# Pooled residual moved from VectorE to ScalarE and GpSimd, and TensorE's loop turned, in a window attention block on one core

## The chip, the core and the metric

The kernel runs on one core of one Trainium2 chip. The metric is the device time of one execution in microseconds. All data is float32. Five engines run side by side, each with its own instruction stream, and meet only through semaphores: TensorE (matmuls into PSUM), VectorE, ScalarE, GpSimd (which here touches SBUF only) and SyncE, which issues the loads and stores.

## What is computed

The input x is 4 x 128 x 96 x 96. It is normalised by groups (32 groups of 4 channels), passed through a multi-scale linear attention within windows of 4 x 4 pixels, and added to itself:

```python
qkv = jnp.einsum('nchw,oc->nohw', xw, qkv_w)       # xw: windows of 4 x 4 pixels
pooled = _avg_pool5(qkv)                           # 5 x 5 mean inside the window
msq = jnp.concatenate([qkv, pooled], axis=1)       # full and pooled branch
q = relu(msq[..., :DIM]); k = relu(msq[..., DIM:2 * DIM]); v = msq[..., 2 * DIM:]
v = jnp.pad(v, ..., constant_values=1.0)           # a column of ones: the denominator
kv = jnp.einsum('ngld,nglm->ngdm', k, v)
out = jnp.einsum('ngld,ngdm->nglm', q, kv)
out = out[..., :-1] / (out[..., -1:] + 1e-15)
y = jnp.einsum('nchw,oc->nohw', out, proj_w)       # then batch norm, scale and shift
x = x + y
```

A 5 x 5 mean inside a 4 x 4 window has only 3 x 3 different values (corners and edges repeat), so the pooled branch is computed on 9 pixels a window instead of 16 and spread out at the very end.

## The kernel before

The image is cut into 96 strips (NS) of 4 rows and 96 columns: 384 pixels (SP), 24 windows, and 216 pooled pixels (SPP). Channels lie on the 128 partitions. The whole input lies in SBUF (x_all), and the result is written over it strip by strip, then stored. Every engine runs its own list over the strips. Those of VectorE, ScalarE and GpSimd are written out for all 96 strips; TensorE's is a loop (line 664) over two strips a round, s = 1, 3, ... 93, with strips 0 and 95 ahead of it and behind it.

TensorE's step for strip s (lines 638 to 651), in this order: kv_products full and pooled (line 582; 48 and 32 matmul passes on 64 x 32 tiles of the array), conv_q (lines 556 and 558), conv_kv of strip s+1 (line 538), transposes of strip s-1 (line 627), conv_kv_pooled of s+1 (line 549), project of s-1 (lines 633 and 635), out_products full and pooled (line 611). Each float32 matmul appears as two passes, each with its weight load.

ScalarE's step (lines 343 to 356): relu of q full and pooled (lines 312, 318), relu of the next k (line 286), evacuation of the transposed outputs o_sb (lines 325, 332), the masked copies of the next v, four full and, behind the relu of the pooled k (line 292), six pooled ones (line 305). The last of the six signals vm_p, for which the pooled kv products wait, together with num_f.

VectorE's step (line 479): own_heads for both branches (line 446, kvc_full and kvc_pool, 2 x 2 instructions), in some strips the statistics of the next image (line 377), residual of strip s-1 (lines 449 to 464), divide for both branches (lines 472, 473, 476; it signals num_f and num_p). residual adds the full part from PSUM bank 0 in one instruction (line 452), and then the pooled part from PSUM bank 1 in four (line 462), one for each pair of kinds of rows and columns. The last signals y_done, for which the store on SyncE waits, and the full kv products two strips on, since they write banks 0 and 1.

GpSimd's step (line 236): the normalisation of strip s+2 into xn (lines 255, 256), which waits for conv_q of strip s (the same half of xn), and eight additions that pool it into xp (line 234).

Of the kernel before, what the change touches and what calls it, by code (L numbers as in the profile page):

```python
# [65 lines left out]
def build(nc, x, wq, wkv, proj, bn, consts, out):  # L66
# [20 lines left out]
    with ExitStack() as ctx:  # L87
# [46 lines left out]
        o_sb = sb("o_sb", [SP + SPP])  # L134

# [42 lines left out]
        added_f = sem("added_f")  # L178
        y_done = sem("y_done")
# [4 lines left out]
        def col(i, n=1):  # L184
            return cst[:, i:i + n]
# [24 lines left out]
        def _(sp):  # L210
# [16 lines left out]
        def _(pool):  # L227
# [51 lines left out]
            over_strips(step)  # L279

        @block.scalar
        def _(act):
# [12 lines left out]
            def masked_v(s, pooled):  # L295
# [37 lines left out]

            def square_root(n):
# [8 lines left out]
            def step(s, b, at, phase):  # L343
# [20 lines left out]
            pooled_out(NS - 1)  # L364

        @block.vector
        def _(dve):
# [48 lines left out]

            dve.memset(dev[:], 0.0).then_inc(y_done, 1)
# [31 lines left out]
            def residual(s):  # L449
# [4 lines left out]
                dve.wait_ge(y_p, s + 1)  # L454
                dve.wait_ge(added_f, s + 1)
                src = ps[:, Y_P, 0:SPP].rearrange("p (w r c) -> p w r c", r=NP, c=NP)
                dst = xs.rearrange("p (r w c) -> p w r c", r=WS, c=WS)
                ends, ends_p, mid, mid_p = slice(0, WS, WS - 1), slice(0, NP, NP - 1), slice(1, 3), slice(1, 2)
                for rows, rows_p in ((ends, ends_p), (mid, mid_p)):
                    for cols, cols_p in ((ends, ends_p), (mid, mid_p)):  # L460
                        part = dst[:, :, rows, cols]
# [67 lines left out]
        def _(pe):  # L529
# [12 lines left out]
            def conv_kv_pooled(s, p):  # L542
                pe.wait_ge(xp_ready, s + 1)

                wait(pe, qm_f, s)
# [16 lines left out]
            def kv_products(s, pooled):  # L562


                k, vm, tiles, wins, bank, done = (
                    (k_pool, vm_pool, TP, EP, KVP, kv_p) if pooled else (k_full, vm_full, TF, EF, KVF, kv_f))
                pe.wait_ge(km_p if pooled else km_f, s + 1)
                pe.wait_ge(vm_p if pooled else vm_f, s + 1)
                if pooled:

                    wait(pe, num_f, s)
                else:

                    wait(pe, y_done, s)

                pe.nop(nofuse=True)
                n = wins * KC
                for t in range(tiles):
                    for r in range(G):
                        rows = slice(H64 * r, H64 * (r + 1))  # L580
                        for i in range(4):
                            last = pe.matmul(ps[Q4 * i:Q4 * (i + 1), bank + r, t * n:(t + 1) * n],  # L582
                                             k[rows, t, Q4 * i:Q4 * (i + 1)], vm[rows, t, :, i, :],
                                             start=True, stop=True)
                last.then_inc(done, 1)

            def out_products(s, pooled):


                q, kvc, done, bank, tiles, wins = (  # L590
                    (q_pool, kvc_pool, out_p, OUTP, TP, WP) if pooled else
                    (q_full, kvc_full, out_f, OUTF, TF, WF))
                pe.wait_ge(qm_p if pooled else qm_f, s + 1)
                pe.wait_ge(kvc_p if pooled else kvc_f, s + 1)
                if not pooled:

                    pe.wait_ge(kvc_p, s + 1)
                elif not is_last(s):

                    pe.wait_ge(km_f, s + 2)  # L600
                    pe.wait_ge(vm_f, s + 2)
                pe.nop(nofuse=True)
                n = QG * KC
                blocks = q[:].rearrange("p n e j -> p n (e j)")
                for t in range(tiles):
                    for e in range(wins):
                        for g in range(G):
                            rows = slice(H64 * g, H64 * (g + 1))
                            for c in range(4):
                                r, w = c // QG, t * QG * wins + c % QG * wins + e  # L610
                                last = pe.matmul(ps[Q4 * c:Q4 * (c + 1), bank + g, t * n:(t + 1) * n],  # L611
# [85 lines left out]
```

## Time and profile before

| | us |
|---|---|
| median of 3 runs (from 928.78 to 931.36) | 930.72 |
| the profiled execution | 930.24 |
| its span, from first to last instruction | 928.3 |

The page gives for each engine its busy time and its share of the span. Busy is not the same as needed: TensorE's matmuls are pipelined and their ends are modelled, so that small gaps count more than the share suggests. PE is TensorE's matmul side, PEld its weight load side, DVE is VectorE, ACT ScalarE, POOL GpSimd. The weight load of the next matmul runs beside the matmul before it. The span has three parts: some 69 us in which the first loads, the first statistics and the first three strips run, 92 regular strips, and about 14 us of the last strip. In the timeline a row begins with its start in us and its duration; where the engine stood idle before it, the time and what ended it follow in brackets ("issue": nothing that the profile shows).

### The profile page before, as it was taken

Reading aid. Unit: us, or ns where it says so; the run is one execution under the profiler, and the core shown is the slowest. Engines: PE = TensorE matmul, PEld = TensorE weight load, DVE = VectorE, ACT = ScalarE, POOL = GpSimd, SP = SyncE. Lnnn points to the kernel's source line nnn. Section 1 sums busy time; section 2 is a strip of 40 time slices with the busy share of each in tenths; the row PEclk is TensorE's granted clock in tenths of the full one; section 3 lists DMA queues with packets and bytes.
Section 4 is the critical chain, followed back from the end, with each engine's and each line's share of the span. In section 5 each row is a group of like instructions: output and inputs, shape, how many; then the busy total and the mean of one; then the engine's idle time right before and its main releaser. Section 6 shows DMA issues by size and latency. Waiting matters only on the chain.

```text
span 928.3 us, 65376 instructions
## 1 busy us (share of the span) xinstructions
PE 873.8 (94%) x29282; PEld 733.4 (79%) x29282; DVE 772.3 (83%) x1625; ACT 609.5 (66%) x1542; POOL 456.0 (49%) x967
## 2 busy tenths in 40 slices
PE   0689999999999999999999999999999999999997
PEld 0578888888888888888888888888888888888885
DVE  7369989998878898998878998999887878787886
ACT  0457676767676767676766667676767676767673
POOL 1545454545454545555554545454545454545550
PEclk9999999999999999999999999999999999999998
DMA  9910000000000000000000000000000000000000
GB/s 378 431 50 17 26 17 26 17 26 17 25 19 25 26 17 26 17 26 17 26 17 26 18 26 17 26 17 27 17 26 17 25 25 18 26 17 26 18 26 27
DMA packets 15893, 38.77 MB, mean 42 GB/s; under 512 B 1888, under 2 KB 14688, under 8 KB 15456
## 3 DMA queue, kind: packets, MB, share of 16 engines
q1 hardware_dynamic: 15840, 38.26, 10.6%
q14 instruction: 44, 0.36, 0.1%
q8 instruction: 9, 0.15, 0.1%
HBM read 19.38 MB, written 18.87 MB: 41 GB/s over the span
## 4 chain that ended last, share of the span: by engine, by line
PE 93%; issue 3%; DVE 2%; POOL 1%; DMA 0%; ACT 0%; DVEq 0%; POOLq 0%
PE ps L611 23%; PE ps L582 19%; PE ps L538 14%; PE ps L549 9%; PE ps L556 9%; PE ps L633 7%; PE ps L627 6%; PE ps L635 4%; PE ps L558 4%; DVE stats L377 1%; DMA x_all<-x 0%; POOL hs L234 0%; DVE kvc_full L446 0%; POOL xp L234 0%; ACT o_sb L325 0%
## 5 line engine op out<-in xcount | busy, mean ns | idle before, releaser
L255 POOL TENSOR_TENSOR xn<-x_all,mean_t 128x384 f32<-128x384 f32 x96 | 79.4, 827 | 393.6 <-PE ps L558 375.1
L305 ACT ACTIVATE vm_pool<-ps,cst 128x256 f32<-128x256 f32 x576 | 225.5, 543 | 0.4 <-PE ps L549 0.4
L446 DVE TENSOR_TENSOR kvc_full<-ps,cst 128x864 f32<-128x864 f32 x192 | 193.7, 1050 | 17.8 <-PE ps L582 17.6
L446 DVE TENSOR_TENSOR kvc_pool<-ps,cst 128x864 f32<-128x864 f32 x192 | 193.2, 1048 | 0.0
L305 ACT ACTIVATE vm_full<-ps,cst 128x384 f32<-128x384 f32 x384 | 192.2, 598 | 0.9 <-PE ps L538 0.9
L312 ACT ACTIVATE q_full<-ps 128x384 f32<-128x384 f32 x96 | 47.2, 491 | 208.5 <-PE ps L556 208.5
L538 PE MATMUL ps<-wkv_sb,xn 128*128 128x128 f32 x1152 | 145.5, 276 | 23.5 <-POOL xn L256 23.5
L538 PEld LDWEIGHTS ps<-wkv_sb,xn 128*128 128x128 f32 x1152 | 144.1, 193 | 23.5 <-issue 23.5
L452 DVE SCALAR_TENSOR_TENSOR x_all<-ps,shift,x_all 128x384 f32<-128x384 f32 x96 | 59.3, 618 | 93.4 <-PE ps L633 93.2
L611 PEld LDWEIGHTS ps<-kvc_full,q_full 64*32 64x32 f32 x9216 | 99.5, 105 | 26.4 <-issue 26.3
L611 PE MATMUL ps<-kvc_pool,q_pool 64*32 64x72 f32 x9216 | 115.8, 230 | 2.1 <-issue 2.1
L611 PE MATMUL ps<-kvc_full,q_full 64*32 64x72 f32 x9216 | 116.5, 230 | 0.9 <-issue 0.9
L582 PE MATMUL ps<-vm_full,k_full 64*32 64x144 f32 x4608 | 95.8, 289 | 21.5 <-issue 20.7
L611 PEld LDWEIGHTS ps<-kvc_pool,q_pool 64*32 64x32 f32 x9216 | 101.5, 105 | 6.7 <-issue 2.4
L549 PE MATMUL ps<-wkv_sb,xp 128*128 128x128 f32 x768 | 102.5, 277 | 0.6 <-POOL xp L234 0.6
L549 PEld LDWEIGHTS ps<-wkv_sb,xp 128*128 128x128 f32 x768 | 94.1, 193 | 0.9 <-POOL xp L234 0.9
L582 PE MATMUL ps<-vm_pool,k_pool 64*32 64x216 f32 x3072 | 94.1, 350 | 0.3
L582 PEld LDWEIGHTS ps<-vm_full,k_full 64*32 64x32 f32 x4608 | 69.5, 106 | 31.5 <-issue 29.2
L234 POOL TENSOR_TENSOR hs<-ht,xn 128x96 f32<-128x96 f32 x192 | 85.6, 446 | 15.1
L556 PE MATMUL ps<-xn,wq_sb 128*128 128x384 f32 x192 | 88.4, 542 | 0.0
L256 POOL TENSOR_TENSOR xn<-xn,rstd_t 128x384 f32<-128x384 f32 x96 | 79.6, 829 | 7.6
L325 ACT ACTIVATE o_sb<-ps 128x384 f32<-128x384 f32 x96 | 47.2, 491 | 53.2 <-PE ps L627 53.2
(66 smaller groups left out, 1242.2 us busy)
## 6 DMA issues: line engine op xcount, KB each, us to landing
out<-x_all SPq DMA_DIRECT2D x96, 192.0 KB, 1.9
x_all<-x SPq DMA_DIRECT2D x3, 4608.0 KB, 32.1
x_all<-x SPq DMA_DIRECT2D x6, 768.0 KB, 8.1
cst<-consts SPq DMA_DIRECT2D x1, 172.0 KB, 11.0
wkv_sb<-wkv SPq DMA_DIRECT2D x1, 128.0 KB, 10.8
o_sb<-proj SPq DMA_DIRECT2D x1, 128.0 KB, 10.4
wq_sb<-wq SPq DMA_DIRECT2D x1, 64.0 KB, 10.5
bn_sb<-bn SPq DMA_DIRECT2D x1, 2.0 KB, 10.3
```

Of the source, the lines that this page charges most:

```text
L234: return pool.tensor_tensor(o, a, b, ALU.add)
L255: link(pool.tensor_tensor(xr, src, mean, ALU.subtract), 1)
L256: pool.tensor_tensor(xn[:, p], xn[:, p], rstd, ALU.mult).then_inc(xn_ready, 1)
L305: last = act.activation(heads[:, :, e, :, 0:D], src, ACT.Copy, scale=col(mask + e))
L446: last = dve.tensor_tensor(kvc[:, g], src.to_broadcast(shape), own, ALU.mult)
L452: dve.scalar_tensor_tensor(xs, ps[:, Y_F, 0:SP], shift[:], xs, ALU.add, ALU.add).then_inc(added_f, 1)
L538: last = pe.matmul(ps[:, bank, t * P:(t + 1) * P], xn[:, p, t * P:(t + 1) * P], wkv_sb[:, half * P:(half + 1) * P], start=True, stop=True)
L549: last = pe.matmul(ps[:, bank, t * P:(t + 1) * P], xp[:, p, t * P:(t + 1) * P], wkv_sb[:, half * P:(half + 1) * P], start=True, stop=True)
L556: pe.matmul(ps[:, Q_F, 0:SP], wq_sb[:], xn[:, p], start=True, stop=True).then_inc(q_f, 1)
L582: last = pe.matmul(ps[Q4 * i:Q4 * (i + 1), bank + r, t * n:(t + 1) * n], k[rows, t, Q4 * i:Q4 * (i + 1)], vm[rows, t, :, i, :], start=True ...
L611: last = pe.matmul(ps[Q4 * c:Q4 * (c + 1), bank + g, t * n:(t + 1) * n], blocks[rows, 4 * t + c, Q4 * e:Q4 * (e + 1)], kvc[rows, r, w], st ...
L633: pe.matmul(ps[:, Y_F, 0:SP], projT[:, 0:P], o_sb[:, 0:SP], start=True, stop=True).then_inc(y_f, 1)
```

## The change

Three things change.

1. The pooled part of the residual leaves VectorE. ScalarE copies PSUM bank 1 (128 x 216) to a new tile y_pool, between the second and the third pooled masked v activation of its step, and signals y_copied. GpSimd then makes the four additions, behind the normalisation in its step, and signals y_done. y_pool is a single buffer: the copy waits for y_done of the strip before.
2. TensorE waits for added_f and y_copied instead of y_done where banks 0 and 1 are written again. Some waits that others imply are dropped.
3. TensorE's loop begins with the next strip's conv_kv and ends with its conv_q; the kv products and conv_q of strip 0 stand ahead of the loop. The cyclic order of the matmuls is the same.

```diff
@@ sync
-                    sp.wait_ge(y_done, t + (b * SPB + 2))
+                    sp.wait_ge(y_done, t + (b * SPB + 1))
@@ gpsimd
+            def residual_pooled(s):
+                pool.wait_ge(added_f, s + 1)
+                pool.wait_ge(y_copied, s + 1)
+                src = y_pool[:].rearrange("p (w r c) -> p w r c", r=NP, c=NP)
+                dst = x_all[:, s * SP:(s + 1) * SP].rearrange("p (r w c) -> p w r c", r=WS, c=WS)
+                ends, ends_p, mid, mid_p = slice(0, WS, WS - 1), slice(0, NP, NP - 1), slice(1, 3), slice(1, 2)
+                for rows, rows_p in ((ends, ends_p), (mid, mid_p)):
+                    for cols, cols_p in ((ends, ends_p), (mid, mid_p)):
+                        part = dst[:, :, rows, cols]
+                        last = add(part, src[:, :, rows_p, cols_p].to_broadcast([P, NW, 2, 2]), part)
+                last.then_inc(y_done, 1)
...
                     normalise_and_pool(s + 2, s % 2)
+                if not is_first(s):
+                    residual_pooled(s - 1)
@@ scalar
                 for e in range(wins):
                     last = act.activation(heads[:, :, e, :, 0:D], src, ACT.Copy, scale=col(mask + e))
+                    if between is not None and e == 1:
+                        copy_y_pooled(between)
                 last.then_inc(done, 1)
...
+            def copy_y_pooled(s):
+                act.wait_ge(y_p, s + 1)
+                wait(act, y_done, s)
+                act.activation(y_pool[:], ps[:, Y_P, 0:SPP], ACT.Copy).then_inc(y_copied, 1)
...
-                    masked_v(s + 1, True)
+                    masked_v(s + 1, True, None if is_first(s) else s - 1)
@@ vector
-                dve.wait_ge(y_p, s + 1)
-                dve.wait_ge(added_f, s + 1)
...
-                        last = dve.tensor_tensor(part, src[:, :, rows_p, cols_p].to_broadcast([P, NW, 2, 2]),
-                                                 part, ALU.add)
-                last.then_inc(y_done, 1)
@@ tensor
             def conv_q(s, p):
-                pe.wait_ge(km_p, s + 1)
...
-                pe.wait_ge(vm_p, s + 1)
...
+            def kv_products(s):
+                wait(pe, added_f, s - 1)
+                wait(pe, y_copied, s - 1)
+                pe.wait_ge(vm_f, s + 1)
+                pe.nop(nofuse=True)
+                for t in range(TF):
+                    last = kv_tile(False, t)
+                last.then_inc(kv_f, 1)
+            def kv_products_pooled(s):
+                pe.wait_ge(vm_p, s + 1)
+                wait(pe, num_f, s)
+                pe.nop(nofuse=True)
+                for t in range(TP):
+                    last = kv_tile(True, t)
+                last.then_inc(kv_p, 1)
...
             def step(s, p):
-                kv_products(s, False)
-                kv_products(s, True)
-                conv_q(s, p)
-                if not is_last(s):
-                    conv_kv(s + 1, 1 - p)
+                conv_kv(s + 1, p)
                 if not is_first(s):
                     transposes(s - 1)
-                if not is_last(s):
-                    conv_kv_pooled(s + 1, 1 - p)
+                conv_kv_pooled(s + 1, p)
                 if not is_first(s):
                     project(s - 1)
-                out_products(s, False)
-                out_products(s, True)
+                out_products(s)
+                out_products_pooled(s)
+                kv_products(s + 1)
+                kv_products_pooled(s + 1)
+                conv_q(s + 1, p)
...
-            step(0, 0)
+            kv_products(0)
+            kv_products_pooled(0)
+            conv_q(0, 0)
+            step(0, 1)
             with pe.Fori(1, NS - 1, 2) as s:
-                step(s, 1)
-                step(s + 1, 0)
-            step(NS - 1, (NS - 1) % 2)
+                step(s, 0)
+                step(s + 1, 1)
+            transposes(NS - 2)
+            project(NS - 2)
+            out_products(NS - 1)
+            out_products_pooled(NS - 1)
```

kv_tile and out_tile hold the matmuls of the old kv_products and out_products, in the same order.

## Rows read from the trace of the kernel before

**Rows 1.** The page: busy us (share of the span) of each engine, granted clock.

```profile
PE 873.8 (94%) x29282; PEld 733.4 (79%) x29282; DVE 772.3 (83%) x1625; ACT 609.5 (66%) x1542; POOL 456.0 (49%) x967
...
PEclk9999999999999999999999999999999999999998
```

**Rows 2.** Waits from 69 to 914 us: total us, times, longest.

```profile
PEld ps L582 <- issue: 33.9, 92, 0.5
...
PE ps L582 <- issue: 15.8, 45, 0.4
```

**Rows 3.** Timeline of an odd step: start us, duration us, engine, line.

```profile
418.40 0.30 PEld L556 LDWEIGHTS ps<-xn,wq_sb 128*128 128x128 f32 x2 [0.34 <-issue]
...
421.38 0.49 ACT L325 ACTIVATE o_sb<-ps 128x384 f32<-128x384 f32 x1 [0.51 <-PE ps L627]
...
421.77 0.34 ACT L332 ACTIVATE o_sb<-ps 128x216 f32<-128x216 f32 x1
...
422.00 2.00 ACT L305 ACTIVATE vm_full<-ps,cst 128x384 f32<-128x384 f32 x4
...
423.87 0.75 DVE L462 TENSOR_TENSOR x_all<-ps,x_all 128x96 f32<-128x96 f32 x4
...
424.12 2.35 ACT L305 ACTIVATE vm_pool<-ps,cst 128x256 f32<-128x256 f32 x6
...
425.38 0.56 DVE L476 TENSOR_TENSOR o_full<-ps,den_full 128x384 f32<-128x384 f32 x1
425.58 0.72 PEld L582 LDWEIGHTS ps<-vm_full,k_full 64*32 64x32 f32 x48
...
426.54 0.58 PEld L582 LDWEIGHTS ps<-vm_pool,k_pool 64*32 64x32 f32 x32 [0.24 <-issue]
...
427.46 0.30 PEld L556 LDWEIGHTS ps<-xn,wq_sb 128*128 128x128 f32 x2 [0.34 <-issue]
```

**Rows 4.** Timeline of the even step that follows it.

```profile
428.40 1.49 PEld L538 LDWEIGHTS ps<-wkv_sb,xn 128*128 128x128 f32 x12
...
428.82 0.83 POOL L255 TENSOR_TENSOR xn<-x_all,mean_t 128x384 f32<-128x384 f32 x1 [3.77 <-PE ps L558]
...
433.18 2.35 ACT L305 ACTIVATE vm_pool<-ps,cst 128x256 f32<-128x256 f32 x6
433.54 1.06 PEld L611 LDWEIGHTS ps<-kvc_pool,q_pool 64*32 64x32 f32 x96
...
435.09 0.72 PEld L582 LDWEIGHTS ps<-vm_full,k_full 64*32 64x32 f32 x48 [0.49 <-issue]
...
435.85 0.58 PEld L582 LDWEIGHTS ps<-vm_pool,k_pool 64*32 64x32 f32 x32
...
436.77 0.30 PEld L556 LDWEIGHTS ps<-xn,wq_sb 128*128 128x128 f32 x2 [0.34 <-issue]
```

**Rows 5.** Timeline: line 556's load at the start of strip 3 and of 95.

```profile
69.06 0.30 PEld L556 LDWEIGHTS ps<-xn,wq_sb 128*128 128x128 f32 x2 [0.34 <-issue]
...
914.31 0.30 PEld L556 LDWEIGHTS ps<-xn,wq_sb 128*128 128x128 f32 x2 [0.34 <-issue]
```

**Rows 6.** Groups by line, GpSimd's small additions: busy us, mean ns, idle before.

```profile
L234 POOL TENSOR_TENSOR hs<-ht,xn 128x96 f32<-128x96 f32 x192 | 85.6, 446 | 15.1
...
L234 POOL TENSOR_TENSOR xp<-vt,hs 128x72 f32<-128x72 f32 x192 | 64.4, 335 | 15.0
...
L234 POOL TENSOR_TENSOR hs<-hs,xn 128x96 f32<-128x96 f32 x96 | 49.6, 517 | 0.0
```

**Rows 7.** Timeline of the end: the last projection and the last residual.

```profile
924.24 0.93 PE L635 MATMUL ps<-o_sb,projT 128*128 128x216 f32 x2
...
925.20 0.75 DVE L462 TENSOR_TENSOR x_all<-ps,x_all 128x96 f32<-128x96 f32 x4
```

**Rows 8.** The page's DMA queues, those that bring instructions: packets, MB, share.

```profile
q14 instruction: 44, 0.36, 0.1%
q8 instruction: 9, 0.15, 0.1%
```

More of the change, by code:

```diff
@@ L134, in build @@
         o_sb = sb("o_sb", [SP + SPP])
+        y_pool = sb("y_pool", [SPP])
         proj_sb = o_sb[:, 0:2 * P]
@@ L178, in build @@
         added_f = sem("added_f")
+        y_copied = sem("y_copied")
         y_done = sem("y_done")
@@ L279, in _ @@
             over_strips(step)
+            residual_pooled(NS - 1)
         @block.scalar
@@ L293, in relu_k_pooled, with masked_v @@
                                ACT.Relu, scale=1 / 25.0).then_inc(km_p, 1)
-            def masked_v(s, pooled):
+            def masked_v(s, pooled, between=None):
                 ready, free, done, bank, vm, tiles, wins, mask = (
@@ L353, in step @@
                     relu_k_pooled(s + 1)
-                    masked_v(s + 1, True)
+                    masked_v(s + 1, True, None if is_first(s) else s - 1)
+                elif not is_first(s):
+                    copy_y_pooled(s - 1)
                 if phase == 2:
@@ L364, in _ @@
             pooled_out(NS - 1)
+            copy_y_pooled(NS - 1)
         @block.vector
@@ L415, in _ @@
             dve.memset(mv[:], 0.0).then_inc(mv_zero, 1)
-            dve.memset(dev[:], 0.0).then_inc(y_done, 1)
             dve.wait_ge(mv_zero, 1)
@@ L453, in residual @@
                                          ALU.add).then_inc(added_f, 1)
-                dve.wait_ge(y_p, s + 1)
-                dve.wait_ge(added_f, s + 1)
[L456 to L461, printed above, removed]
-                        last = dve.tensor_tensor(part, src[:, :, rows_p, cols_p].to_broadcast([P, NW, 2, 2]),
-                                                 part, ALU.add)
-                last.then_inc(y_done, 1)
             def divide(s, pooled):
@@ L543, in conv_kv_pooled @@
                 pe.wait_ge(xp_ready, s + 1)
-                wait(pe, qm_f, s)
                 wait(pe, qm_p, s)
@@ L560, in conv_q @@
                           start=True, stop=True).then_inc(q_p, 1)
[L562 to L602, printed above, removed]
+            def kv_tile(pooled, t):
+                k, vm, bank, n = (k_pool, vm_pool, KVP, EP * KC) if pooled else (k_full, vm_full, KVF, EF * KC)
+                for r in range(G):
+                    rows = slice(H64 * r, H64 * (r + 1))
+                    for i in range(4):
+                        last = pe.matmul(ps[Q4 * i:Q4 * (i + 1), bank + r, t * n:(t + 1) * n],
+                                         k[rows, t, Q4 * i:Q4 * (i + 1)], vm[rows, t, :, i, :],
+                                         start=True, stop=True)
+                return last
@@ L603, in out_products, with out_tile @@
+            def out_tile(pooled, t, e):
+                q, kvc, bank, wins = (q_pool, kvc_pool, OUTP, WP) if pooled else (q_full, kvc_full, OUTF, WF)
                 n = QG * KC
                 blocks = q[:].rearrange("p n e j -> p n (e j)")
[L605 to L611, printed above, removed]
-                                                 blocks[rows, 4 * t + c, Q4 * e:Q4 * (e + 1)], kvc[rows, r, w],
-                                                 start=e == 0, stop=e == wins - 1)
@@ L614, in out_products @@
-                last.then_inc(done, 1)
+                for g in range(G):
+                    rows = slice(H64 * g, H64 * (g + 1))
+                    for c in range(4):
+                        r, w = c // QG, t * QG * wins + c % QG * wins + e
+                        last = pe.matmul(ps[Q4 * c:Q4 * (c + 1), bank + g, t * n:(t + 1) * n],
+                                         blocks[rows, 4 * t + c, Q4 * e:Q4 * (e + 1)], kvc[rows, r, w],
+                                         start=e == 0, stop=e == wins - 1)
@@ new lines, in out_tile @@
+                return last
+            def kv_products(s):
[13 more added lines that the diff above has]
+                last.then_inc(kv_p, 1)
@@ new lines, in out_products, with out_products_pooled @@
+            def out_products(s):
+                if is_last(s):
+                    pe.wait_ge(qm_p, s + 1)
+                pe.wait_ge(kvc_p, s + 1)
+                pe.nop(nofuse=True)
+                for t in range(TF):
+                    for e in range(WF):
+                        last = out_tile(False, t, e)
+                last.then_inc(out_f, 1)
+            def out_products_pooled(s):
+                if not is_last(s):
+                    pe.wait_ge(vm_f, s + 2)
+                    pe.nop(nofuse=True)
+                for t in range(TP):
+                    for e in range(WP):
+                        last = out_tile(True, t, e)
+                last.then_inc(out_p, 1)
@@ L616, in transposes @@
             def transposes(s):
-                pe.wait_ge(num_f, s + 1)
-                pe.wait_ge(num_p, s + 1)
                 if not is_last(s):
@@ L622, in transposes @@
                 else:
-                    pe.wait_ge(y_done, s + 1)
+                    pe.wait_ge(num_p, s + 1)
+                    pe.wait_ge(added_f, s)
+                    pe.wait_ge(y_copied, s)
                 for bank, o, n, pxs, columns, done in (
```

## The prediction

> **What bounds the kernel now.** I read the page's engine lines first. TensorE is busy for 94% of the span and nearly always at its full granted clock; VectorE has 83%, ScalarE 66%, GpSimd 49% [rows 1]. So the time is TensorE's step, repeated 96 times. The next view is the chain of waits between strip 3 and strip 94: TensorE's weight loads stand still 92 times ahead of line 582, up to 0.5 us each, but its matmuls idle there in only 45 of the 92 steps, 15.8 us in all [rows 2]. Two kinds of step alternate, then, and the timeline shows both.
>
> The odd step runs from the weight load of line 556 at 418.40 to the next at 427.46: 9.06 us [rows 3]. Loads of the full kv products begin at 425.58, those of the pooled ones at 426.54. The load of 48 tiles takes 0.72 us, so the pooled loads could have begun at about 426.34: 0.20 us are lost. What arrives last is ScalarE's pooled masked v: six activations from 424.12 for 2.35 us, ending at 426.47, and the loads begin 0.07 us later. VectorE's o_full, the other thing waited for, ended at 425.94. ScalarE's chain has no hole: from the evacuation o_sb at 421.38, which waits for the transposes of line 627, to 426.47 each activation follows the one before [rows 3]. The loop TensorE transposes, ScalarE 5.09 us, TensorE pooled kv, convolutions, transposes therefore sets the odd step.
>
> The even step, 427.46 to 436.77, is 9.31 us [rows 3, 4]. Here masked v ends at 433.18 + 2.35 = 435.53, the same 8.07 us into the step, but the full kv loads begin only at 435.09, 7.63 us in instead of 7.18, and the pooled ones follow at 0.76 us with no wait. The first matmul load has 0.49 us of idle time that the profile puts down to issue: this is where TensorE's loop of two strips jumps back. It costs 0.45 us at that point and 0.25 us net, since 0.20 us of it lies over the wait for ScalarE. The mean of the two is 9.185 us; the 92 steps from 69.06 to 914.31 took 845.25 us [rows 5], 9.188 each.
>
> **The jump moved.** In the new order the jump comes behind conv_q and ahead of the next conv_kv. The cyclic order of all matmuls stays as it was. Behind conv_q TensorE has its four long passes in hand: from the first load at 427.46 to the first load of line 538 at 428.40 are 0.94 us [rows 3, 4], with the last pass still running. The jump's gap of 0.49 us was measured behind the out products, where a load and its matmul together take 11 ns (1.06 us for 96) and little is in hand. I take it as covered. If the cover fails, the gap stands in front of the convolution and pushes the transposes and ScalarE's whole chain with it. Taking the 0.45 us away from the full kv products gives back no more than 0.25 us in each even step, as then the pooled ones wait for ScalarE as in the odd step. With all else as before each step would be 9.06 us: 92 x 9.06 = 833.5, or 11.7 us less.
>
> **The copy on ScalarE.** One activation of 128x216 from PSUM is put between the second and the third of the six pooled masked v activations, so in front of the signal that already arrives last. Its price on a saturated ScalarE is the distance of starts, not the duration. The same shape, line 332, lasts 0.34 us, and the next activation starts 0.23 us after it (421.77 to 422.00); at 384 elements, line 325, it is 0.39 us (421.38 to 421.77) [rows 3]. Both have semaphore waits behind them too, so satisfied waits cost nothing beyond this. I take 0.235 us, by the row of the same shape; the lower bound is 0.23, the upper the full 0.344, if nothing overlaps. Every step is then 9.06 + 0.235 = 9.295 us: 92 x 9.295 = 855.1 us, that is 9.9 us more than 845.25. The upper bound gives 9.404 and 865.2, 20 us more. The break-even is a copy of 0.125 us.
>
> The Trainium skill ("ScalarE: Activation LUTs", What ACT_TABLE_LOAD costs) gives an activation with immediate operands 186 ns plus 0.833 ns an element and an overlap of 93 ns between neighbours, which as an estimate makes 273 ns for this copy, a step of 9.33 us and 3.5 us more than my sum. The trace has the same shape at 344 ns and 230 ns from start to start, so its numbers are used.
>
> **What VectorE loses and GpSimd gets.** Four adds of line 462 leave VectorE: 0.75 us from 423.87 to 424.62 [rows 3]. Nothing that ends last comes sooner: o_full was already 0.53 us ahead of masked v. In the few steps with group statistics, where VectorE runs late, it saves tenths in all. GpSimd gets four adds of 128x96. Its rows for near shapes are 335 ns (72 elements), 446 and 517 ns (96 elements, two inputs) [rows 6], so between 1.3 and 2.1 us; I take 1.8. They begin once the copy is done, about 5.72 (424.12 less 418.40) + 2 x 0.39 (2.35 over six) + 0.34 = 6.84 us into the step, and end by 8.9. GpSimd had 3.77 us idle before its next subtraction, which starts 1.36 us into a step (428.82) [rows 4], so about 10.6 on this scale. 1.7 us of slack remain; behind GpSimd's new waits stand the normalisation of a later strip, which has a whole step in hand, and the store. Covered, at nothing. Should the adds take more than 3.7 us they would delay the normalisation, and later the convolutions.
>
> **New and dropped waits of TensorE.** The full kv products wait for added_f and y_copied in place of y_done. The copy is done at 6.84 us and the loads start at 7.18: with the 0.07 us of a hand-over 0.27 us of slack, cost nothing; if it were later, both kv products and conv_q, queued behind, would slip with it. ScalarE's copy waits for y_p, whose matmul comes ahead of the out products in TensorE's order, and for y_done of the strip before, done in the step before. The dropped waits (km_p, vm_p ahead of conv_q, num_f and num_p ahead of the transposes, qm and kvc_f ahead of the out products) were met long before: no gap stands there but the 0.34 us in which loads wait for a change from 64x32 tiles to the full array, and that change stays. Nothing, below as above. SP's stores leave about 2.5 us later in each step, hidden except for the last.
>
> **The ends.** At the start only the even step 2 has a jump (-0.25 us). Behind the last projection VectorE's four adds took from 925.20 to 925.95 with the y_p matmul ending at about 925.17 [rows 7]. Now: copy 0.34 us and GpSimd's 1.8 us with two hand-overs of some 0.07 us, until about 927.45: +1.5 us (bounds +1.0 to +1.8). Sum: 9.9 - 0.25 + 1.5 = 11.1 us, span 928.3 + 11.1 = 939.4, and with the 1.9 us around the span 941.3. The profiled execution, 930.24, lies 0.5 us under the median of 930.72; I name 941.5.
>
> **Rivals.** (a) *The jump isn't covered.* It then puts 0.25 to 0.45 us in front of the convolution in every other step, which ScalarE's chain can't absorb since it starts behind: 46 x 0.25 to 0.45 = 11.5 to 20.7 us on top, 953 to 962. For it speaks that the profile names only "issue" and doesn't say how far TensorE's instructions run ahead; against it the four long passes, and that no code is fetched again in a round: the two instruction queues carry 53 packets for all engines and the whole run, against 47 rounds of TensorE's loop alone with over 1200 matmul and load instructions each [rows 1, 8].
> The Trainium skill ("Runtime: NRT & Kernel Launch", Instruction fetch mechanics) says that a jump whose target lies outside the current window forces a fetch before execution goes on; by it the new jump would stall like the old one, wherever it stands, which is rival (a). The packet count speaks against such a fetch here.
> (b) *Faster: ScalarE's copy isn't what the pooled kv products wait for.* The start 0.07 us behind masked v would then be a coincidence with some fixed cost, the copy would be free and only the jump's gain remain: -11.7 + 1.25 gives about 920. It decides once the copy delays line 582 by less than 0.11 us per step. Against it: in the even step the same waits stand there and cost nothing, once masked v is early.
> (c) *GpSimd or the single y_pool buffer becomes the bound*: only with adds of over 0.9 us each, twice any row; then each 0.1 us beyond costs 9 us, 950 and more.
> (d) *The jump's stall doesn't go away at all but stays hidden beside the copy*: this differs from the forecast by less than 2 us, since the new start, 8.14 (426.54 less 418.40) + 0.235 = 8.375 us into the step, is as late as the old even one at 8.39.
>
> **How the numbers follow.** Forecast with (d) 0.73, from 938 to 951 by the copy's bounds; (a) 0.10; (b) 0.13; (c) 0.04. A measurement of this kernel can tell about 0.3% (2.8 us) from no change. Partial forms of (b), a copy of around 0.11 us, get 0.03 of it for "same"; so faster 0.10, same 0.03, slower 0.87. The range 934 to 954 leaves out (b), most of (a) and part of (c), some 2 in 10. At the upper bound of the copy the sum is 951.4; 934 leaves room for starts of code and a copy a little cheaper.
>
> **What will show it.** In the profile after: all steps alike at about 9.30 us; no matmul idle ahead of the full kv products; pooled kv loads starting 0.07 us behind the last masked v, with about 0.4 us of idle before them in every step, against 0.24 in odd ones now; ScalarE's masked v row x6 split by a 0.34 us copy and ending 8.3 us into the step; VectorE under 76% busy, GpSimd near 65%; GpSimd still idle before its subtraction. Wrong would be: idle time ahead of line 538's loads (rival a), pooled kv loads not tied to ScalarE (b), or GpSimd without idle time (c).

## The result and the profile after

The changed kernel takes 945.58 us (median of four executions, 942.66 to 946.69) against 930.73 us: 1.0158 times as long, 95% interval 1.0131 to 1.0186. I had predicted 941.5 us. The profiled execution has a span of 943.6 us against 928.3. One execution of the kernel of experiment 1 took 4563.85 us, about five times its others; no trace of it is kept, and the ratio there leaves it out.

Read in the same order as before, first the page: engine lines, the two queues that bring instructions, the chain that ended last by engine, and the costliest group.

```profile
PE 869.7 (92%) x29282; PEld 727.4 (77%) x29282; DVE 696.5 (74%) x1240; ACT 631.4 (67%) x1638; POOL 604.8 (64%) x1351
...
q14 instruction: 45, 0.37, 0.1%
q8 instruction: 9, 0.15, 0.1%
...
PE 42%; ACT 37%; issue 17%; DVE 2%; POOL 1%; DMA 0%; ACTq 0%; POOLq 0%; DVEq 0%
...
L323 ACT ACTIVATE vm_pool<-ps,cst 128x256 f32<-128x256 f32 x576 | 242.7, 549 | 0.4 <-PE ps L563 0.4
```

The matmuls are busy for less time than before [rows 1] in a longer span. The chain that ended last runs through ScalarE for 37% of it, where the kernel before has PE 93% and ACT 0%. The waits from 69 to 920 us (total us, times, longest), against [rows 2]:

```profile
POOL xn L257 <- PE ps L570: 198.4, 91, 4.9
...
PEld ps L581 <- issue: 58.7, 92, 2.0
...
POOL x_all L236 <- ACT y_pool L357: 32.8, 91, 0.7
PE ps L581 <- ACT vm_pool L323: 32.5, 91, 0.4
```

Line 581 is the old line 582. TensorE's matmuls now idle ahead of the kv products in every step, and the profile names ScalarE's masked v as what ends it, where it had named nothing ("issue") in every second step. That the name appears isn't the copy's doing, however. The same row of two later runs, first the turned loop without any copy (experiment 1), then the changed kernel with one old wait of TensorE put back (experiment 7, `after_km`):

```profile
PE 42%; ACT 39%; issue 14%; DVE 4%; POOL 1%; DMA 0%; ACTq 0%; DVEq 0%; POOLq 0%
```

```profile
PE 92%; issue 4%; DVE 2%; POOL 1%; DMA 0%; ACT 0%; POOLq 0%; DVEq 0%
```

The second waits for ScalarE as long as the changed kernel does, but for 0.03 us a step, and its chain doesn't show it. So these shares can't say which engine a step waits for; the positions in the timeline can. GpSimd still waits for TensorE: it is not a bound.

One step in the timeline (start, duration), to be laid beside [rows 3, 4]:

```profile
425.86 0.30 PEld L569 LDWEIGHTS ps<-xn,wq_sb 128*128 128x128 f32 x2 [0.34 <-issue]
...
426.80 1.49 PEld L553 LDWEIGHTS ps<-wkv_sb,xn 128*128 128x128 f32 x12
...
428.84 0.49 ACT L345 ACTIVATE o_sb<-ps 128x384 f32<-128x384 f32 x1 [0.51 <-PE ps L655]
...
431.57 0.89 ACT L323 ACTIVATE vm_pool<-ps,cst 128x256 f32<-128x256 f32 x2
...
432.29 0.41 ACT L357 ACTIVATE y_pool<-ps 128x216 f32<-128x216 f32 x1
...
432.51 1.64 ACT L323 ACTIVATE vm_pool<-ps,cst 128x256 f32<-128x256 f32 x4
432.84 0.56 DVE L491 TENSOR_TENSOR o_full<-ps,den_full 128x384 f32<-128x384 f32 x1
432.84 1.57 POOL L236 TENSOR_TENSOR x_all<-y_pool,x_all 128x96 f32<-128x96 f32 x4 [0.36 <-ACT y_pool L357]
432.93 0.72 PEld L581 LDWEIGHTS ps<-vm_full,k_full 64*32 64x32 f32 x48
...
434.27 0.58 PEld L581 LDWEIGHTS ps<-vm_pool,k_pool 64*32 64x32 f32 x32 [0.62 <-issue]
...
435.19 0.30 PEld L569 LDWEIGHTS ps<-xn,wq_sb 128*128 128x128 f32 x2 [0.34 <-issue]
...
436.13 1.49 PEld L553 LDWEIGHTS ps<-wkv_sb,xn 128*128 128x128 f32 x12
```

The step is 9.33 us, and every other one from strip 3 on is 9.33 or 9.34. ScalarE's chain begins 2.98 us into the step, as before, and ends at 432.51 + 1.64 = 434.15, 8.29 us in, where it was 8.07; the copy is the 0.22 us (432.29 to 432.51). VectorE's o_full ended at 433.40, long before. The pooled kv loads begin 0.12 us behind masked v, not 0.07. GpSimd's additions take 1.57 us beside all this. The full kv loads have no idle time in front, and neither have the convolution's first loads (line 553), which start 0.94 us behind conv_q's in steps with a jump between them and in steps without, as in the kernel before. The jump's stall is gone, but the step is no shorter for it.

### The profile page after: what moved, and what is told of

Same layout as the page of the kernel before. It is cut to its first block, busy times and chain, and to the rows that moved or that the text cites. A ratio compares the mean times of both kernels' runs of the same rounds, so it can differ in the third digit from the quotient of the medians.

```text
span 943.6 us, 65183 instructions
## 1 busy us (share of the span) xinstructions
PE 869.7 (92%) x29282; PEld 727.4 (77%) x29282; DVE 696.5 (74%) x1240; ACT 631.4 (67%) x1638; POOL 604.8 (64%) x1351
## 4 chain that ended last, share of the span: by engine, by line
PE 42%; ACT 37%; issue 17%; DVE 2%; POOL 1%; DMA 0%; ACTq 0%; POOLq 0%; DVEq 0%
ACT vm_pool L323 18%; PE ps L553 13%; ACT vm_full L323 12%; PE ps L581 10%; PE ps L569 9%; ACT y_pool L357 4%; PE ps L570 4%; PE ps L655 4%; ACT k_pool L310 3%; DVE stats L405 1%; PE ps L596 1%; PE ps L563 1%; DMA x_all<-x 0%; ACT o_sb L352 0%; ACT o_sb L345 0%
## 5 line engine op out<-in xcount | busy, mean ns | idle before, releaser
L323 ACT ACTIVATE vm_pool<-ps,cst 128x256 f32<-128x256 f32 x576 | 242.7, 549 | 0.4 <-PE ps L563 0.4
L236 POOL TENSOR_TENSOR x_all<-y_pool,x_all 128x96 f32<-128x96 f32 x384 | 150.1, 428 | 50.5 <-ACT y_pool L357 50.5
L581 PEld LDWEIGHTS ps<-vm_pool,k_pool 64*32 64x32 f32 x3072 | 56.9, 107 | 60.0 <-issue 59.6
## 6 DMA issues: line engine op xcount, KB each, us to landing
cst<-consts SPq DMA_DIRECT2D x1, 172.0 KB, 11.1
```

What stands on the lines that cost most here:

```text
L236: return pool.tensor_tensor(o, a, b, ALU.add)
```

## The experiments

Steps are given from one weight load of conv_q's first matmul to the next, positions as us into such a step. Where two or more edits make up a kernel, the diffs name the lines that matter, and "..." marks lines left out. Where a ratio is given, the time is a median of four executions or more, compared with the kernel before in the same session; the other times are those of one execution, and there the steps of the trace carry the argument.

**1. The loop alone.** The changed kernel with the pooled residual back on VectorE:

```diff
-                wait(pe, added_f, s - 1)
-                wait(pe, y_copied, s - 1)
+                wait(pe, y_done, s - 1)
...
+                        last = dve.tensor_tensor(part, src[:, :, rows_p, cols_p].to_broadcast([P, NW, 2, 2]),
+                                                 part, ALU.add)
+                last.then_inc(y_done, 1)
```

> Only TensorE's loop is turned (and its waits thinned as in the change); the pooled residual stays on VectorE, with no copy and no additions on GpSimd. My theory (the pooled kv products wait for ScalarE's last masked v, and a jump behind conv_q costs nothing): every step is as long as an odd step of before, 9.06 us, 92 steps take 833.5 us in place of 845.3, and the time is about 919 (917 to 922). Rival a (the jump's 0.25 to 0.45 us isn't covered behind conv_q): every second step 9.31 to 9.5 us, 930 to 940 us. Rival of a fixed hand-over that grew with the new waits: 0.05 us a step more, 9.11 us and 924.

Measured: 923.98 us, 0.994 of the kernel before (0.992 to 0.996): a gain of 0.6%. Of the 92 regular steps 91 are 9.09 or 9.10 us; one, in which VectorE averages the groups, is 9.39.

```profile
430.97 2.35 ACT L307 ACTIVATE vm_pool<-ps,cst 128x256 f32<-128x256 f32 x6
...
433.43 0.58 PEld L573 LDWEIGHTS ps<-vm_pool,k_pool 64*32 64x32 f32 x32 [0.44 <-issue]
433.46 0.96 PE L573 MATMUL ps<-vm_pool,k_pool 64*32 64x216 f32 x32 [0.18 <-ACT vm_pool L307]
```

No step is held up by the jump (rival a is out), and the time it had cost is won back but for 0.04 us a step: masked v ends at 433.32, the loads start 0.11 us later. So the 917 to 922 us that I expected were missed, by the longer hand-over, the last of the alternatives that I had named.

**2. The move alone.** The kernel before, with the copy on ScalarE and the additions on GpSimd, TensorE's order untouched:

```diff
-                    wait(pe, y_done, s)
+                    wait(pe, added_f, s)
+                    wait(pe, y_copied, s)
```

> Only the pooled residual is moved (ScalarE's copy between the second and third pooled masked v, four additions on GpSimd); TensorE's loop begins and ends where it did. Theory: masked v ends 0.22 us later than before, so odd steps are about 9.28 to 9.33 us; in even steps the jump's stall (pooled kv loads not before 8.39 us) and the copy's wait (8.37 to 8.41) lie over each other, so they are about 9.31 to 9.34. Time about 942 to 946, the same as the whole change: the turned loop bought nothing beside the copy. If the two stalls added up instead, even steps would be 9.55 us and the time about 955.

Measured: 941.8 us, 0.2 us below the expected range, 1.0125 of before (1.0108 to 1.0142). Odd steps are 9.29 us, even ones 9.31 or 9.32. An odd and the next even step:

```profile
430.69 1.65 ACT L323 ACTIVATE vm_pool<-ps,cst 128x256 f32<-128x256 f32 x4
...
432.40 0.58 PEld L601 LDWEIGHTS ps<-vm_pool,k_pool 64*32 64x32 f32 x32 [0.47 <-issue]
...
439.98 1.64 ACT L323 ACTIVATE vm_pool<-ps,cst 128x256 f32<-128x256 f32 x4
...
440.95 0.72 PEld L601 LDWEIGHTS ps<-vm_full,k_full 64*32 64x32 f32 x48 [0.50 <-issue]
...
441.72 0.58 PEld L601 LDWEIGHTS ps<-vm_pool,k_pool 64*32 64x32 f32 x32
```

In the even step the jump's 0.50 us and the wait for the later masked v (439.98 + 1.64 = 441.62) end together. So the copy is nearly the whole loss, and beside it the turned loop has nothing to give. The 92 steps take 855.9 us here and 858.7 in the changed kernel; experiment 7 shows where the other 2.8 us come from.

**3. The copy left out.** GpSimd adds a tile of zeros instead, so this kernel leaves the pooled residual out of its result.

```diff
-                pool.wait_ge(y_copied, s + 1)
...
-                    masked_v(s + 1, True, None if is_first(s) else s - 1)
+                    masked_v(s + 1, True)
```

> The changed kernel without ScalarE's copy; GpSimd still makes its four additions each strip, but from a y_pool that is zero, so the pooled residual is left out of the result. TensorE waits for added_f only. Theory (copy in front of the last masked v is the whole price): 9.06 us a step, about 920 to 922 us. Rival (the price is GpSimd's additions, or the copy's wait for them): stays near 9.33 us and 943 to 946. If only the longer hand-over to TensorE is left: 9.11 us and about 925.

Measured: 924.17 us, steps of 9.10 or 9.11 us.

```profile
422.66 2.35 ACT L323 ACTIVATE vm_pool<-ps,cst 128x256 f32<-128x256 f32 x6
423.52 1.57 POOL L237 TENSOR_TENSOR x_all<-y_pool,x_all 128x96 f32<-128x96 f32 x4
...
425.12 0.58 PEld L578 LDWEIGHTS ps<-vm_pool,k_pool 64*32 64x32 f32 x32 [0.48 <-issue]
```

GpSimd's additions are all there, at 1.57 us, and cost no step anything. This is the result of experiment 1 again, whoever adds, and again about 0.04 us a step over an odd step of before, which I had named as the alternative (about 925).

**4. The copy doubled.**

```diff
+                act.activation(y_spare[:], ps[:, Y_P, 0:SPP], ACT.Copy)
                 act.activation(y_pool[:], ps[:, Y_P, 0:SPP], ACT.Copy).then_inc(y_copied, 1)
```

> The changed kernel with a second copy of the same 128x216 by ScalarE, into a tile that nobody reads, ahead of the one into y_pool. Theory: the price is the distance of starts on a saturated ScalarE, so a second copy adds 0.23 to 0.25 us to each step: 9.56 to 9.58 us, 92 steps 21 to 23 us more than the changed kernel, 966 to 970 us. The full kv products start later too (y_copied about 0.24 us later, at 7.1 us) without ending last. Rival (there is slack behind, or the first copy paid for a wait and not for its length): less than 0.1 us a step, under 955 us.

Measured: 969.3 us, steps of 9.57 or 9.58 us, 0.24 more than with one copy, as expected.

```profile
433.48 0.41 ACT L358 ACTIVATE y_spare<-ps 128x216 f32<-128x216 f32 x1
433.71 0.42 ACT L359 ACTIVATE y_pool<-ps 128x216 f32<-128x216 f32 x1
433.94 1.65 ACT L324 ACTIVATE vm_pool<-ps,cst 128x256 f32<-128x256 f32 x4
```

Each copy lasts 0.41 us here and moves the next start by 0.23 us. The step pays the distance of starts and not the duration.

**5. The copy behind all of masked v.**

```diff
-                    if between is not None and e == 1:
-                        copy_y_pooled(between)
...
+                if not is_first(s):
+                    copy_y_pooled(s - 1)
```

> The changed kernel with ScalarE's copy behind all six pooled masked v activations instead of behind the second. Masked v is then signalled as early as in the kernel before (8.06 us), but y_copied, for which the full kv products wait (they write the PSUM bank that the copy reads), comes at about 8.25 us instead of 6.84. Theory: full kv loads start at 8.35 instead of 7.07, pooled ones 0.65 us later at 9.0, steps of 9.9 to 9.95 us, time 997 to 1004: with this bank shared, each place of the copy costs, and the one of the change is the cheaper. Rival (the wait for y_copied ends nothing, only masked v does): 9.10 us a step and 924.

Measured: 1009.58 us, 5.6 us above the expected range; steps of 10.03 or 10.04 us.

```profile
427.48 2.34 ACT L323 ACTIVATE vm_pool<-ps,cst 128x256 f32<-128x256 f32 x6
429.62 0.45 ACT L357 ACTIVATE y_pool<-ps 128x216 f32<-128x216 f32 x1
430.13 0.72 PEld L581 LDWEIGHTS ps<-vm_full,k_full 64*32 64x32 f32 x48 [1.34 <-issue]
430.16 0.98 PE L581 MATMUL ps<-vm_full,k_full 64*32 64x144 f32 x48 [1.19 <-ACT y_pool L357]
```

Now the full kv products wait for the copy, which still reads the bank that they write. The mechanism is the expected one. The copy ends 8.30 us into the step (I had 8.25), the full and the pooled loads start at 8.36 and 9.01 (8.35 and 9.0); from the pooled loads to the next step are 1.02 us, and I had 0.90 to 0.95. That tail is the miss.

**6. The copy on VectorE.** The changed kernel, with the copy behind VectorE's full residual:

```diff
+                dve.wait_ge(y_p, s + 1)
+                wait(dve, y_done, s)
+                dve.tensor_copy(y_pool[:], ps[:, Y_P, 0:SPP]).then_inc(y_copied, 1)
```

> The changed kernel with one thing else: the copy into y_pool is made by VectorE, behind its full residual, instead of by ScalarE. GpSimd still adds, the loop is still turned. Theory: ScalarE's chain is as short as before, so steps are 9.10 us as in the run with the turned loop alone (9.05 us to masked v's end plus 0.12 and the rest), time 923 to 925: the move to GpSimd itself costs nothing in the steps, and gains nothing either, since VectorE didn't end last. Rival (GpSimd's additions, or the hand-over between three engines, are part of the price): above 927.

Measured: 924.66 us, 0.9939 of before (0.9922 to 0.9957); steps of 9.10 or 9.11 us. Off ScalarE the same copy, and with it the whole move to GpSimd, is free, and worth nothing either: the turned loop alone takes 9.09 or 9.10 us a step.

**7. One wait put back**, in the kernel of experiment 1 (`turned_km`) and in the changed kernel (`after_km`):

```diff
             def kv_products_pooled(s):
+                pe.wait_ge(km_p, s + 1)
                 pe.wait_ge(vm_p, s + 1)
```

> The run with only the loop turned, plus TensorE's old wait for km_p (the pooled relu of k, done 2 us earlier) ahead of its wait for vm_p in the pooled kv products. There the loads start 0.11 to 0.12 us behind the end of masked v, in the kernel before and in the one with only the residual moved 0.07. Theory that the dropped wait is what changed the hand-over: 0.07 again, steps of 9.05 to 9.06 us, about 4 us less, 919 to 920. Rival (it comes from something else in the turned order, as the code position): stays at 0.11 and 9.10 us, 923 to 925.

> The changed kernel with TensorE's old wait for km_p put back ahead of its wait for vm_p in the pooled kv products. In the kernel with the turned loop this brought the hand-over from 0.11 to 0.07 us. Theory: the same here, steps of 9.29 us in place of 9.335, 92 steps 4 us less, time 939 to 943. Then the step that my prediction undersized is this hand-over and not the copy. Rival: 9.33 us and 944 to 947.

Measured: 918.24 and 939.24 us. By the timeline's rounded starts, steps are 9.06 (76 of 92) and 9.30 us (72 of 92), nearly all others 0.01 us beside. From the first:

```profile
419.02 2.35 ACT L307 ACTIVATE vm_pool<-ps,cst 128x256 f32<-128x256 f32 x6
...
421.44 0.58 PEld L573 LDWEIGHTS ps<-vm_pool,k_pool 64*32 64x32 f32 x32 [0.43 <-issue]
```

Masked v ends at 421.37 and the loads begin 0.07 us later, as in the kernel before. One more wait, long since met, placed before the one that isn't met yet makes the hand-over 0.04 us shorter: 92 x 0.035 = 3.2 us in the changed kernel. All the other kernels agree: 0.07 us with this wait (the kernel before and that of experiment 2, in the steps that wait for ScalarE), 0.11 to 0.12 without it (experiments 1, 3, 4, 6 and 8). The profiled execution without that wait took 945.41; the other 3 us of the difference lie ahead of strip 3, which began at 68.2 us in place of 71.2. Why the extra wait helps the traces don't show.

**8. ScalarE relieved.** Experiment 6, and the pooled outputs evacuated by VectorE too:

```diff
-                    pooled_out(s - 1)
...
+            def pooled_out(s):
+                dve.wait_ge(tr_p, s + 1)
+                wait(dve, y_p, s)
+                dve.tensor_copy(o_sb[:, SP:], ps[:, TRP, 0:SPP]).then_inc(o_p, 1)
```

> Built to beat both: TensorE's loop turned; the pooled residual copied from PSUM by VectorE (one copy of 216 in place of four additions) and added by GpSimd; and the pooled half of ScalarE's output evacuation (line 352 of the changed kernel, 128x216) moved to VectorE, so that ScalarE's chain in front of the pooled kv products is 0.23 us shorter than before. Theory: masked v ends about 7.83 us into a step, pooled kv loads start at 7.94, steps of 8.86 to 8.90 us, 92 steps about 816 us, time 902 to 906 us; in strips with statistics VectorE (about 8.9 us of work a step) may hold a step up by 0.1 to 0.2 us, which gives up to 912. If ScalarE's chain weren't what the pooled kv products wait for, the steps stay at 9.10 us and the time at 922 to 925.

Measured: 903.77 us, 0.9703 of before (0.9677 to 0.9728), all 92 steps at 8.86 or 8.87 us. An activation of 0.23 us taken away from the chain gives 0.24 us a step, the mirror image of the change.

**9. The chain shortened by order alone**: the first of the full masked v ahead of o_sb, on the kernel of experiment 8, on that of experiment 1, and on that of experiment 1 with VectorE evacuating the pooled outputs.

```diff
                     relu_k(s + 1)
+                    masked_v(s + 1, False, part=slice(0, 1))
                 if not is_first(s):
                     to_image(s - 1)
...
-                    masked_v(s + 1, False)
+                    masked_v(s + 1, False, part=slice(1, None))
```

> The fastest kernel so far (turned loop; VectorE copies y_pool and evacuates the pooled outputs; GpSimd adds) with one reordering on ScalarE: the first of the four full masked v activations stands ahead of the evacuation o_sb, in the 0.5 us in which ScalarE waits for the transposes. Theory: o_sb starts some 0.13 us later, but the chain behind it is one activation (0.46 us) shorter, masked v ends about 7.5 us into a step in place of 7.83, and the pooled kv products no longer wait for ScalarE: TensorE alone sets a step of 8.63 to 8.67 us, 92 steps 794 to 798 us, time 881 to 886 us. Rival (VectorE becomes the bound in strips with statistics, where it had 0.6 us of idle time in 8.87): up to 890. Rival (the delayed o_sb holds up the projection): steps above 8.75 us and over 890.

> The same reordering on the kernel with only the loop turned (residual and outputs where they were before the change). Theory: masked v ends 0.33 us earlier, 7.73 us into a step, pooled kv loads start at 7.85, steps of 8.77 to 8.79 us, 92 steps 807 to 809 us, time 893 to 897. If VectorE's later o_full (7.54 us into a step) or the delayed o_sb ended last instead, the steps would stay above 8.9 us.

> Turned loop, the first full masked v ahead of o_sb, the pooled outputs evacuated by VectorE, but the pooled residual left on VectorE as in the kernel before: no y_pool, no additions on GpSimd. It asks what the move to GpSimd is worth once ScalarE no longer ends last. Theory: VectorE has 0.45 us more work a step than with the copy; in the 60 strips without statistics it still fits into 8.65 us, in the 36 with them it comes to about 8.75 us: time 884 to 889, 0 to 4 us more than with GpSimd. Rival (VectorE's four additions push o_full behind and hold the pooled kv products in every step): 8.8 us and more, 895 or above.

Measured: 891.46 us, 0.9581 of before (0.9565 to 0.9597); 895.8; 890.47. From the first:

```profile
430.94 0.58 ACT L323 ACTIVATE vm_full<-ps,cst 128x384 f32<-128x384 f32 x1 [0.18 <-PE ps L561]
...
431.42 0.48 ACT L346 ACTIVATE o_sb<-ps 128x384 f32<-128x384 f32 x1
```

The second came as expected (8.77 us in 71 of 92 steps by the timeline's rounded starts). The first missed by 5 us: its steps are 8.73 to 8.77 us, not 8.65. ScalarE doesn't end last any more (masked v ends 7.50 us in, the pooled loads start at 7.71 to 7.75), VectorE neither (o_full 7.54). The number is that of the rival in which the later o_sb holds up the projection, but the out products behind the projection start 5.00 us into the step as in the kernel before, so it is not that.

What is left is TensorE's own order, and there the kernel without y_copied starts its full kv products at 6.96 us and has steps of 8.66 us, against 7.07 to 7.10 and 8.74 to 8.77. The latter has one wait more ahead of them. These two kernels differ in more than that wait, but the other traces bear it out. Counted from the second half of the out products, the full kv loads start after 0.99 us (in nearly every step) in the five turned kernels without y_copied (experiments 1, 3, 7 first kernel, 9 second and third), and after 1.10 to 1.14 us in the five with it (the changed kernel, experiments 6, 7 second kernel, 8, 9 first; in experiments 4 and 5 the copy itself comes too late), even where VectorE's copy ended at 5.65 us, long before. The number of waits alone isn't the rule: the kernel before has three there and that of experiment 2 has four, and both take 1.10 us. Why 65 of the 92 steps take 8.76 or 8.77 us and the others 8.73 to 8.75 stays open.

The third, one execution, lies 1.5 us above its expected range. Without GpSimd the six strips in which VectorE averages the groups take 9.46 to 9.75 us, since o_full is late there, and this eats up most of the advantage. Its 92 steps still take 3.2 us less than those of the first (802.5 against 805.7); the times are within 1 us of each other because its strip 3 began 2.7 us later (71.96 against 69.29). So in this order GpSimd's additions aren't worth the wait that they bring.

## Why the prediction was right, and where it was off

The mechanism was the predicted one: the copy stands in the chain that the pooled kv products wait for, and every step pays for it. The sum was 9.9 (steps) - 0.25 (start) + 1.5 (end) = 11.1 us of span. The trace has 15.3: its regular steps run from 71.19 to 929.87 us.

```profile
70.30 0.54 PEld L581 LDWEIGHTS ps<-vm_pool,k_pool 64*32 64x32 f32 x30 [2.04 <-issue]
...
71.19 0.30 PEld L569 LDWEIGHTS ps<-xn,wq_sb 128*128 128x128 f32 x2 [0.34 <-issue]
...
929.87 0.30 PEld L569 LDWEIGHTS ps<-xn,wq_sb 128*128 128x128 f32 x2 [0.34 <-issue]
```

**The steps** took 858.7 us, 13.4 more than before [rows 5], where I had 9.9. *The copy on ScalarE* was sized rightly: 0.22 to 0.24 us for my 0.235 (the step after, experiment 4). Of the missing 3.5 us 3.2 are the hand-over from ScalarE to TensorE, which I had carried over at 0.07 us from [rows 3] and which became 0.12. The term that was off is in the part on dropped waits: "Nothing, below as above". Removing TensorE's wait for km_p, which I had placed ahead of conv_q only, also touched the pooled kv products, and cost 0.035 us a step; putting it back brought the steps to 9.30 us. Other dropped waits did shorten something: with the loop turned the out products' second half starts at 5.97 us in place of 6.08 [rows 4], and the full kv products at 7.07 or, without y_copied, at 6.96, in place of 7.18 [rows 3]. That lay hidden behind ScalarE.

**The jump** went as predicted: no idle time ahead of the convolution, every step like an odd one, 0.25 us net in every second step, and this disappears as soon as the copy stands there (experiments 1 and 2). Rival (a) is ruled out. The Trainium skill ("Runtime: NRT & Kernel Launch", Instruction fetch mechanics) has a jump fetch code if its target is out of the current window. The trace shows no such fetch in each round of this loop: its two instruction queues carry 54 packets for all engines, and there are 47 rounds. The rule itself isn't tested by that, as no run shows whether the target was in the window.

**The start** was predicted at -0.25 and was +2.1 us. The 2.04 us of issue above, in the middle of strip 3's pooled kv products, is a stop that the kernel before hasn't got there. All twelve kernels with the loop turned have it at this place, 1.2 to 2.3 us long, and neither of the two without (the kernel before and that of experiment 2). With the loop turned, more instructions run for the first time ahead of the second round. That the stop is a wait for code is my reading, and two things speak for it: its code runs for the first time there only in the turned order (in the old one the round repeats strip 1's), and TensorE's stops of over 0.8 us from 38 us on, this one the last, lie 127, 252, 252 and 126 weight loads apart, as if code came in pieces of one size. The start as a whole varies with more than this stop: strip 3 begins at 68.2 us in one turned kernel and at 72.8 in another, and at 70.5 in that of experiment 2, whose loop isn't turned. So I leave open how much of the 2.1 us is the change's.

**The end** was predicted at +1.5 and was -0.2 us. The residual behind the last projection did cost what I said; after, then the last projection of before:

```profile
938.00 0.91 PE L661 MATMUL ps<-o_sb,projT 128*128 128x384 f32 x2 [0.36 <-ACT o_sb L345]
...
938.75 0.53 PE L663 MATMUL ps<-o_sb,projT 128*128 128x216 f32 x2
...
939.31 0.35 ACT L357 ACTIVATE y_pool<-ps 128x216 f32<-128x216 f32 x1 [1.13 <-PE ps L663]
...
939.80 1.54 POOL L236 TENSOR_TENSOR x_all<-y_pool,x_all 128x96 f32<-128x96 f32 x4 [4.31 <-ACT y_pool L357]
```

```profile
922.88 1.56 PE L633 MATMUL ps<-o_sb,projT 128*128 128x384 f32 x2 [0.36 <-ACT o_sb L325]
```

From the last pooled matmul's end to the last addition are 2.06 us (939.28 to 941.34) against 0.78 [rows 7], 1.3 more. That term was sized rightly, but the last projection took 1.28 us in place of 2.29. Over the last 14 us the mean granted clock was 1.00 after and 0.81 before, and over the last projection of before 0.53, most of it at the lower of the two levels (1.2 GHz, against 2.4):

```profile
914.30:928.30 14.00, 8.45 (x222) 5.52 (x214) 8.21 (x20) 2.21 (x6) 0.00 (x0) 0.81 0.09 31
...
922.88:925.17 2.29, 2.28 (x4) 1.09 (x4) 0.62 (x1) 0.19 (x1) 0.00 (x0) 0.53 0.00 0
```

```profile
929.90:943.60 13.70, 7.31 (x220) 5.07 (x214) 6.30 (x12) 2.91 (x8) 3.10 (x8) 1.00 0.13 45
```

Ahead of that projection TensorE's matmuls had been idle for 1.39 us and, after the transposes, for 0.36 us, and after the change for 1.34 and 0.36. The clock at the end isn't the change's doing as far as the runs show: the last projection took 2.25 us in the kernel of experiment 1 and 1.28 in the same kernel with one wait more (experiment 7), with granted clocks of 0.80 and 1.00 over their last 14 us.

The three errors are +3.5 us in the steps, +2.4 at the start and -1.7 at the end. That the total came within 4.1 us is in part luck: the clock at the end took off 1.0 us which no term of mine foresaw.

**The other rivals.** (b), that ScalarE isn't what the pooled kv products wait for, falls with experiments 3, 4 and 8: take the copy away, double it, or take another activation away, and the step follows by 0.23 to 0.24 us each time. (c), GpSimd as the bound: its additions took 1.57 us (I had 1.8) and it still waited for TensorE 91 times. (d), the stall hidden beside the copy, isn't what happens in the changed kernel, where the stall is gone; experiment 2 is that case, and its steps are within 0.04 us of the changed kernel's. (d) allowed less than 2 us in all; the steps differ by 2.8, by the dropped wait. The figure of the Trainium skill ("ScalarE: Activation LUTs", What ACT_TABLE_LOAD costs), 273 ns for the copy, is above the 220 to 240 ns measured. The step of 9.33 us that it would give is the measured one by coincidence: the rest of it is the hand-over.

## What to carry to other kernels

Before work is moved off an engine, ask which engine's chain ends last at the wait that TensorE really makes, and not which engine is busiest: here VectorE had 83%, ScalarE 66%, and the change that put 0.23 us a step onto the less busy one cost 1.6%, while 0.23 us moved off it and one reordering took another 3.6% off (924.66 to 891.46 us). Two stalls in one step that end at about the same time hide each other, so removing one is worth only the distance to the other. A wait that looks superfluous is part of the change when it is dropped: the one dropped ahead of the pooled kv products cost 3.2 us. An activation on a saturated ScalarE costs the distance between starts, and the idle time of the engine in front of a wait is the place for work that is already there.

## What the runs showed of the hardware

- A wait that is met long before isn't always free or always a cost on TensorE: one more of them ahead of a wait not yet met made the start behind it 0.04 us earlier (experiment 7), and the turned kernels, with fewer waits between groups of 64x32 tiles, started the second half of the out products 0.11 us earlier (0.97 us behind the first half, not 1.08), and those without y_copied the full kv products by another 0.11 us (experiment 9). Three and four waits there took the same 1.10 us.
- TensorE's jump, 0.45 us behind short matmuls, cost nothing behind four passes that take 0.94 us from their first load to the first load behind them (experiment 1).
- GpSimd adds 128x96 float32 elements in 0.39 us each in a row of four (1.57 us), beside VectorE's work and without slowing it: o_full takes 0.56 us and ends 7.54 us into a step with and without them.
